# Attention scores computed head by head in row tiles and moved between partitions, in place of logits from mixed queries

## What is computed

```python
q, k = conv1x1_bn(xn, ...)            # 8 heads of 32 channels
v4 = conv1x1_bn(xn, ...)              # 8 heads of 128 channels
vl = depthwise_conv3x3(v4) * lv_s + lv_t
attn = einsum('bhid,bhjd->bhij', q, k) * 32 ** -0.5
attn = attn + ab[:, BIAS_IDXS]
attn = einsum('bhij,gh->bgij', attn, th1w) + th1b   # mixes the 8 heads
attn = softmax(attn)
attn = einsum('bhij,gh->bgij', attn, th2w) + th2b   # mixes them again
o = relu(einsum('bhij,bhjd->bhid', attn, v) + vl)
out = x + conv1x1_bn(o, pw, ...)
```

## Time and profile before

| | us |
|---|---|
| median of 3 runs (4534.37 to 4536.29) | 4536.19 |
| the profiled execution | 4534.58 |
| its span | 4532.8 |
| TensorE busy | 4505.5 (99%) |
| VectorE busy | 4197.4 (93%) |
| ScalarE busy | 3570.3 (79%) |
| GpSimd busy | 1360.9 (30%) |

### The profile page before, as it was taken

One profiled execution on the slowest core, in us unless ns is written; L12 is line 12 of the kernel. 1 busy time (PEld: TensorE's weight loads), 2 busy tenths in 40 slices (PEclk: granted clock), 3 DMA queues, 4 the chain that ended last, 5 costly groups with the idle time before them and its releaser, 6 DMA issues.

```text
span 4532.8 us, 108461 instructions
## 1 busy us (share of the span) xinstructions
PE 4505.5 (99%) x33666; PEld 4502.5 (99%) x33666; DVE 4197.4 (93%) x10015; ACT 3570.3 (79%) x8508; POOL 1360.9 (30%) x1288
## 2 busy tenths in 40 slices
PE   7999999999999999999999999999999999999999
PEld 7999999999999999999999999999999999999999
DVE  8999999999999999999999999999999999999998
ACT  7787877878778787787787877878778778787786
POOL 2323323323233232332322323323233232332322
PEclk9999999999999999999999999999999999999999
DMA  3322222223222232222322322223222232232222
GB/s 94 97 65 81 86 69 87 65 81 92 70 81 74 72 97 65 81 82 68 93 65 81 88 72 82 68 78 97 65 81 79 67 97 65 81 86 68 88 65 76
DMA packets 211502, 356.05 MB, mean 79 GB/s; under 512 B 15843, under 2 KB 132691, under 8 KB 211413
## 3 DMA queue, kind: packets, MB, share of 16 engines
q1 hardware_dynamic: 211478, 355.75, 27.3%
HBM read 199.71 MB, written 155.98 MB: 78 GB/s over the span
## 4 chain that ended last, share of the span: by engine, by line
PE 99%; DMA 0%; POOL 0%; DVE 0%; SPq 0%; ACT 0%; issue 0%; POOLq 0%; DVEq 0%
PE psA L293 45%; PE psA L426 15%; PE psL L293 13%; PE psM L293 10%; PE psM L404 9%; PE psL L404 7%; PE psA L306 0%; DMA qa<-in_wqkv 0%; SPq L254 0%; POOL xs L822 0%; DVE probs L730 0%; DMA by_key<-probs 0%; POOL wp_lo L863 0%; DVE q_lo L722 0%; ACT w_hi L443 0%
## 5 line engine op out<-in xcount | busy, mean ns | idle before, releaser
L700 DVE SCALAR_TENSOR_TENSOR psC<-vpad,par,psC 128x406 f32<-128x406 f32 x3072 | 1807.2, 635 | 0.0
L584 ACT ACTIVATE probs<-probs,nmax 112x196 f32<-112x196 f32 x1792 | 803.2, 451 | 128.8 <-DVE nmax L759 112.9
L293 PE MATMUL psA<-x_hi,w_lo 128*128 128x392 f32 x2304 | 794.9, 345 | 6.0 <-DVE x_lo L679 6.0
L293 PE MATMUL psA<-x_hi,w_hi 128*128 128x392 f32 x2304 | 785.7, 341 | 0.0
L293 PE MATMUL psA<-x_lo,w_hi 128*128 128x392 f32 x2304 | 785.1, 341 | 0.0
L426 PE MATMUL psA<-qa,shared 105*128 105x196 f32 x4096 | 690.9, 329 | 0.0
L426 PEld LDWEIGHTS psA<-qa,shared 105*128 105x128 f32 x4096 | 677.2, 190 | 0.4 <-DVE shared L794 0.3
L857 POOL TENSOR_TENSOR k_lo<-qk,k_hi 128x392 fp32r<-128x392 f32 x128 | 159.9, 1249 | 1636.4 <-ACT k_hi L490 1636.4
L722 DVE SCALAR_TENSOR_TENSOR q_lo<-qk,th,q_hi 128x392 fp32r<-128x392 f32 x1024 | 618.3, 632 | 2.0 <-ACT q_hi L486 1.9
L486 ACT ACTIVATE q_hi<-qk,th 128x392 fp32r<-128x392 f32 x1024 | 594.5, 618 | 2.1
L461 ACT ACTIVATE o_hi<-shared 128x392 fp32r<-128x392 f32 x512 | 271.6, 530 | 391.3 <-DVE shared L794 391.3
(11 more groups left out here) (85 smaller groups left out, 10723.1 us busy)
## 6 DMA issues: line engine op xcount, KB each, us to landing
by_key<-probs SPq DMA_DIRECT2D x512, 224.0 KB, 3.6
qa<-by_key SPq DMA_DIRECT2D x128, 448.0 KB, 4.3
qk<-by_key SPq DMA_DIRECT2D x128, 448.0 KB, 6.9
xs<-in_x SPq DMA_DIRECT2D x64, 588.0 KB, 3.8
shared<-in_x SPq DMA_DIRECT2D x64, 588.0 KB, 3.8
out<-shared SPq DMA_DIRECT2D x63, 588.0 KB, 3.0
qa<-in_wqkv SPq DMA_DIRECT2D x3, 768.0 KB, 7.1
stage_wp<-in_wp SPq DMA_DIRECT2D x1, 1536.0 KB, 9.6
```

Source lines behind the costliest of these rows:

```text
L293: last = nc.tensor.matmul(dst, w, r, start=(begin and n == 0), stop=(end and n == 2))
L584: nc.scalar.activation(row, row, ACT.Exp, bias=nmax[:, img, b:b + 1], scale=-1.0, accum_out=rowsum[:, img, b:b + 1]).then_inc(s_exp, 1)
L700: nc.vector.scalar_tensor_tensor(a if tap == 7 else sums, src, taps[:, c, TAPS[tap]:TAPS[tap] + 1], a if tap == 0 else sums, MUL, ADD).the ...
```

## The change

The first head mixing is no longer folded into the query. The query is scaled and written with its columns outermost. For each image and each group of 8 or 6 query columns (a unit; four per round) TensorE computes plain scores head by head: eight fp32 matmuls, each on 32 partitions (one head's channels), neighbouring ones on different quarters of the partitions and into different banks. The units stand between the V tiles 2 to 5. ScalarE and VectorE copy two banks of each unit to `scores`, whose partitions are (query column, query row) and whose free dimension holds head and key. SP then moves them within SBUF, eight DMAs per unit, to `by_head`, whose partitions are (head, query column). There one fp32 matmul of 392 columns with `kron1` mixes the heads for two query rows: 14 matmuls per round, the three projection tiles standing after the fourth, eighth and twelfth. `q_hi`, `q_lo`, `k_hi`, `k_lo` are gone.

The transposed V now goes to the buffer `qa` and is stored channel tile innermost; it comes back from DRAM straight into `vt`, whose weights attention times V reads with a stride of eight elements. The copies `head_major` and the reload of the row of ones are gone. The units of attention times V alternate the images, and all of them wait for the last copy of the mixed probabilities. The statistics for the next images, the centres and the convolution steps have new places; 22 convolution steps stand after the second reciprocal and up to eight between the additions.

```diff
-        q, k = qk[:, 0, :, :], qk[:, 2, :, :]
+        by_head = shared[0:HP, heads_at:heads_at + 2 * RES * PIX].rearrange("p (i n) -> p i n", i=2)
+        q, k = qk[:, 0, :, :], qk[:, 1, :, :]
+        scores = qa[0:WIDE, :].rearrange("p (i c h n) -> p i c h n", i=2, c=2, h=NH)
+        turned = qa[:, 0:TURNED].rearrange("p (i b n c) -> p i b n c", i=2, b=BLOCKS, c=VT)
...
+            def moves(t, u):
+
+                img, c = UNITS[u]
+                sp.wait_ge(s_score_a, 8 * t + 2 * u + 2)
+                sp.wait_ge(s_score_v, 8 * t + 2 * u + 2)
+                first_col = c * WIDE // RES
+                for h in range(NH):
+                    lo = h * RES + first_col
+                    sp.dma_start(by_head[lo:lo + score_rows(c) // RES, img, :].rearrange("w (b j) -> w b j", b=RES),
+                                 scores[0:score_rows(c), img, c, h, :]).then_inc(s_moved[u], 16)
+
+            def keys_in(t, img):
+
+                wait_alone(sp, s_vt_out[img], OUTS * (t + 1))
+                sp.wait_ge(s_logit_mm, 14 * t + (14 if img else 11))
+                for jc in range(2):
+                    sp.dma_start(vt[0:ROWS, img, jc, :],
+                                 by_key[img, jc * HALF:jc * HALF + ROWS, :]).then_inc(s_vt_in, 16)
...
-                turned_out(t)
-                ones_in(t)
-                keys_in(t)
+                if first:
+                    sp.wait_ge(s_bias, 1)
+                else:
+                    sp.wait_ge(s_olo, 8 * t)
+                    wait_alone(sp, s_av_mm, 8 * t)
+                for u in range(4):
+                    moves(t, u)
+                turned_out(t, 0)
+                turned_out(t, 1)
+                keys_in(t, 0)
+                keys_in(t, 1)
...
+            def head_scores(t, first, u):
+
+                img, c = UNITS[u]
+                if u:
+                    pe.wait_ge(s_score_a, 8 * t + 2 * u)
+                    pe.wait_ge(s_score_v, 8 * t + 2 * u)
...
+                at_ = img * PIX + c * WIDE
+                for kt in range(QT):
+                    for r in range(QUADS):
+                        part_ = slice(r * KD, (r + 1) * KD)
+                        mm = nc.tensor.matmul(score_bank(r)[0:score_rows(c), kt * PIX:(kt + 1) * PIX],
+                                              q[part_, kt, at_:at_ + score_rows(c)],
+                                              k[part_, kt, img * PIX:(img + 1) * PIX], start=True, stop=True)
+                mm.then_inc(s_score_mm, 1)
...
                     qkv_tile(m, 4 + m).then_inc(s_v_mm, 1)
+                    if m < 6:
+                        head_scores(t, first, m - 2)
...
-                else:
-                    project(t, 0, True)
-                    project(t, 1, True)
...
+                    if n % 7 == 0:
+                        pe.wait_ge(s_moved[2 * img], MOVES * (t + 1))
+                        pe.wait_ge(s_moved[2 * img + 1], MOVES * (t + 1))
                     if n >= 4:
                         pe.wait_ge(s_score, 28 * t + 2 * n - 6)
...
-                    for b in (b0, b0 + 1):
-                        for kt in range(QT):
...
+                    nc.tensor.matmul(logit_bank(n)[:, 0:2 * PIX], kron1[:, :, :].rearrange("p g i -> p (g i)"),
+                                     by_head[:, img, b0 * PIX:(b0 + 2) * PIX], start=True, stop=True
+                                     ).then_inc(s_logit_mm, 1)
...
+                    if n in (3, 7, 11) and not first:
...
+                        project(t, n // 4, True)
...
+                pe.wait_ge(s_vt_in, 64 * (t + 1))
+                pe.wait_ge(s_mix_sb, 14 * t + 14)
+                for u in range(8):
+                    n, img = divmod(u, 2)
...
+                            weights = vt[0:HALF, img, jc, :].rearrange("p (m c) -> p c m", c=VT)
...
+                for u in range(4):
+                    values(2 + u)
+                    score_copy(t, u, 0)
+                    score_copy(t, u, 1)
...
-                CENTRES = {1: 4, 3: 5, 9: 6, 11: 7}
+                CENTRES = {8: 4, 11: 5, 23: 6, 25: 7}
...
+                    if n in (7, 15) and not first:
+                        projected(t, n // 8)
...
+                    if use == 0:
+                        act.wait_ge(s_vt_out[0], OUTS * (t + 1))
+                        act.wait_ge(s_vt_out[1], OUTS * (t + 1))
+                        act.wait_ge(s_moved[2], MOVES * (t + 1))
...
+                convs(13)
...
+                for u in range(4):
+                    score_copies(u)
+                    convs(2 if u < 3 else 3)
...
+                    if n in (3, 7):
+                        turn(n // 4)
+                        convs(2)
+                    if n == 11:
+                        convs(5)
...
-                    convs(1)
                 convs(3)
                 dve.wait_ge(s_exp, 28 * t + 28)
                 nc.vector.reciprocal(rinv[:, 1, :], rowsum[:, 1, :]).then_inc(s_rinv, 1)
-                convs(3)
-                convs(64)
+                convs(22)
...
+                    if u == 6:
+                        convs(64)
...
                     if u:
                         low(u - 1)
+                    convs(1)
```

More of the change, by code:

```diff
@@ L87, in build @@
         proj = sb("proj", [P, CT, COLS])
[L89 to L92, removed]
+        qk = sb("qk", [P, 2, QT, COLS])
+        unused = sb("unused", [P, 2, RUN])
         qa = sb("qa", [P, 4 * RES * HP])
@@ L103, in build @@
         stage_wp = sb("stage_wp", [P, VT * COLS])
-        q_lo = over("q_lo", [P, 2 * RES, QT, HP], VT // 2 * ACC)
-        shared = sb("shared", [P, VT * ACC + 4 * DH + GAP + CT * COLS])
+        shared = sb("shared", [P, VT * ACC + 4 * DH + CT * COLS])
         psA = ctx.enter_context(nc.psum_tensor("psA", [P, 2, BANK], f32))
@@ L387, in step @@
                         pe.wait_ge(s_stat, 4 * (t + 1))
                         group_sums(t + 1)
-                if not first:
-                    project(t, 2, True)
-                pe.wait_ge(s_ones_in, 16 * (t + 2))
+                    if n in (3, 7, 11) and not first:
+                        if n == 7 and not last:
+                            pe.wait_ge(s_gs, t + 2)
+                        project(t, n // 4, True)
+                if first:
+                    pe.wait_ge(s_ones_in, 16)
@@ L448, in _, with conv_centre @@
             weights_high(2)
-            def conv_centre(t, c):
+            def conv_centre(t, first, c):
                 act.wait_ge(s_v_sb, VT * t + c + 1)
+                if not first and c % 2 == 0:
+                    act.wait_ge(s_olo, 8 * (t - 1) + c + 2)
                 if c >= VT // 2:
-                    act.wait_ge(s_logit_mm, 14 * t + c - 3)
+                    act.wait_ge(s_logit_mm, 14 * t + c - 2)
                 src = vpad[:, c, PITCH + 1:PITCH + 1 + ACC_ROWS * PITCH].rearrange("p (r w) -> p r w", w=PITCH)
@@ L527, in step @@
                 values(0)
-                if not first:
-                    act.wait_ge(s_olo, 8 * t)
-                conv_centre(t, 0)
+                conv_centre(t, first, 0)
                 values(1)
-                conv_centre(t, 1)
+                conv_centre(t, first, 1)
+                query_or_key(0)
+                query_or_key(1)
+                query_or_key(2)
+                query_or_key(3)
                 if first:
@@ L854, in step @@
             def step(t, first, last):
-                for kt in range(QT):
-                    wait_alone(pool, s_khi, 2 * t + kt + 1)
-                    nc.gpsimd.tensor_tensor(k_lo[:, kt, :], k[:, kt, :], k_hi[:, kt, :].bitcast(f32),
-                                            SUB).then_inc(s_klo, 1)
                 if first:
```

290 lines of the change are left out of this document (106 added, 184 removed).

## The result

The changed kernel takes 5390.12 us (median; 5385.06 to 5392.25) against 4535.78 of the kernel before in the same runs: 1.188 times as long, 95% interval 1.186 to 1.190, or 854 us, 13.6 us for each of 63 rounds. Forecast were 5090 us and a range of 4620 to 6400. The sign, the wait for the moves as the main loss, and the range came out. Of the two waits that were forecast there is one, and 300 us more were lost than the sum had.

The account below looks back on a forecast made before the run. TensorE, busy 99%, was taken to bound the kernel at 70.2 us per round. The new round, 73.4 us plus 5.6 of waits, makes 79.0, 8.8 more; 63 such add 554 us, giving 5090, range 4620 to 6400.

Parts of the forecast that it names:

- TensorE's list was the bound before, and the change takes little from it: TensorE's work per round: 70.2 us before, 69.2 after, a saving of one microsecond.
- only neighbouring matmuls overlap: Head scores: a second fp32 pass waits for its first, so the scores take 6.4 us per round.
- Two waits for the moves: TensorE waits at the first and eighth mixing, 2.4 and 3.2 us, with moves at 100 GB/s.
- the rival by partitions: Move rate proportional to destination partitions: 50 GB/s gives 103.6 us rounds, 60 to 65 gives 97, 6200 us; chance 0.26.
- the rival with a long pause: Moves at 50 GB/s, late by 14.7 and 15.5 us; clock at 0.50 adds 3 us: rounds of 107, 6850 us.
- From the first mixing to the next round's first tile 47.8 us: Stretch from first mixing until VectorE's add 6 releases the next tile: 47.8 us, against 43.7 for TensorE alone.
- The forecast sign, a TensorE wait of 3 to 4 us at the turn of the round: Before the next round's first tile, TensorE waits 3 to 4 us, released by VectorE's add.
- VectorE covers it: Strided V weight load, between nothing and 2.8 us per round, taken as nothing because VectorE's wait hides it.
- the walk: Step-by-step timing of TensorE, VectorE and ScalarE from the first mixing on; each V unit costs VectorE 1.51 us.
- moves hidden: Moves faster than 130 GB/s cause no wait: rounds of 73.4 us, 4736 us in all; chance 0.24.
- Serial tiles: Score tiles one after another, 10.6 us, leave only a 2.5 us wait: rounds of 80.2, 5160 us; within the forecast's 0.36.
- Faster: Score row tiles fully concurrent, 2.7 us, and moves hidden: rounds of 69.7 us, 4500 us; chance 0.11.

Follow-up runs that it names:

- run 7: Changed kernel with projections 0 and 1 ahead of the first mixing, projection 2 behind mixing 6, ten more convolution steps before the first score row: 5110.85 us, 1.127.
- run 4: Changed kernel whose 32 transfers, from the second round on, keep their packet count but carry a quarter of the bytes: 5190.89 us, 1.145.
- Run 10: Changed kernel with 36 more matmuls a round, whose results nobody reads, ahead of the first mixing: 5318.78 us, 1.173.
- run 1: Changed kernel with the weights of attention times V read packed, from neighbouring elements, instead of with a stride: 5371.6 us, 1.185.
- run 3: Changed kernel moving only head 0 of eight from the second round on, 4 transfers per round in place of 32: 4744.72 us, 1.046.
- run 5: Changed kernel with all head-score matmuls reading partitions 0 to 31, so that they share a row group and run serially: 5587.33 us, 1.233.
- run 11: Changed kernel with the last score unit's eight moves issued by ScalarE's queue, the other 24 by the sync queue: 5495.91 us, 1.212.
- 2: Changed kernel with the earlier kernel's V path: packed transposes, raw buffers, four ScalarE copies, packed weights: 5355.15 us, 1.181.
- 8: Changed kernel with projections 0 and 1 ahead of the first mixing and the earlier kernel's V path together: 5188.79 us, 1.145.

## Why the prediction was right, and where its sum was off

*TensorE's list was the bound before, and the change takes little from it.* Right. 12 tiles and scores take 23.7 us, predicted 25.6; the four units take 3.5 us (0.86 each), not 6.4, but each tile behind one takes 1.81 us in place of 1.61 (2037.16 to 2038.97), 0.8 in all, which the sum didn't have. What failed is that because of the two passes "only neighbouring matmuls overlap": in the timeline all four tiles are at work in either pass. The Trainium skill (TensorE: Matmul & The Clock Gate, Part 3) has 3.07 for 512 columns, by which the prediction estimated 3.5 us; the trace agrees.

*Two waits for the moves, 2.4 and 3.2 us.* The sum, 5.6, against 7.2 to 7.7 and no second one. TensorE is at the first mixing 1.9 us earlier than reckoned (the scores), and units 0 and 1 land 30.7 us after the first tile, not 28.0, though the rate over all four units was close: 2.46 MB in 24.3 us of issue, 101 GB/s, against 100 taken, and units 2 and 3 land after 41.4 us (run 7), not 40.3. That the rate came out was luck, as its reason was another. I took it from the number of partitions; run 4 shows the issue of 32 transfers as the cap and the bytes as a tail of 6 us behind it, which I had at 0.7. From 27.6 GB/s for four partitions in the Trainium skill (SBUF — State Buffer, Door 1) the prediction estimated 55 for eight; the windows between 2050.4 and 2062.4 show 101 to 133, with several transfers to different partitions under way, so the rival by partitions falls.

*The half clock.* Missing in the sum: 2.2 us a round. I had it for the rival with a long pause, from the earlier trace rows, and not for my own pauses of 2 to 3 us; the pause became one of 7. Run 10 shows the mechanism.

*From the first mixing to the next round's first tile 47.8 us.* Measured 52.1 (2056.00 to 2108.06). 2.2 of the 4.3 are the clock. The other 2.0 are in the tail: by TensorE's count the strided weights make 15.6 us of attention times V, where the sum had 13.4; by VectorE's, as run 1 shows, the low half beside GpSimd's `x_lo` makes 15.3. Each alone brings the 2 us, and each hides the other. The forecast sign, a TensorE wait of 3 to 4 us at the turn of the round for VectorE's add, isn't there: TensorE is busy for all 15.62 us, so it is the load that VectorE's tail hides behind, and "VectorE covers it" failed for a load that costs 5.0 us a round, above my bound of 2.8. Taking it away gains 18 us in all, but only because of the second failed term, VectorE's tail: the changed order brings `x_lo` for the next images (2.7 us on GpSimd) beside the low halves, and the walk had only waits for semaphores. In run 1 VectorE needs 12.6 us from its first add to the end of the one that the next tile waits for, against 10.8 by the walk. The transposes' 3.4 us were not priced at all and cost nothing that shows.

The ledger for one round: 79.0 predicted, +1.6 wait, -1.9 scores, +2.2 clock, +2.0 tail makes 82.9, and the round above has 82.94; of the 0.7 by which the mean round is longer, 0.5 are the wait (7.7 on the mean). The rival *moves hidden*, 4736, was met by run 3 within 9 us, by luck: a round of run 3 takes 73.40 us against 73.4, but from 23.5 up to the first mixing in place of 25.6, and 49.9 behind it in place of 47.8, so that the scores' error and the tail's cancel. *Serial tiles* would have been 5587, not 5160 (run 5): 2.8 us a unit as priced, but the granted clock falls in the last ones, so that TensorE is at the first mixing after 36.2 us and not 29.8; the second wait of 2.5 isn't there, and the tail is 49.9 again. *Faster* was never near: even with moves hidden the kernel is at 4745.

What stays open: what besides the issue holds the moves back (run 11); whether the same bytes in fewer transfers would land earlier, which no run tried; and why the granted clock falls under serial matmuls on 32 rows.

## What to carry to other kernels

A transfer between partitions in many small DMAs had two prices here, one for each issue, which a quarter of the payload didn't lower, and a landing time behind the last, which it did; work out both against the first instruction that needs the data, and keep independent work to stand in that gap. A pause on TensorE can also cost what comes after it, at half clock: 2.2 us behind 7.2 here. Undoing one part of a change can gain next to nothing (1, 2: 18 and 35 us) because another engine's work has the same length, and undoing two can be worse than one (8): a part is worth what the next wait leaves.

## What the hardware showed that I had not expected

- Four row tiles of fp32 matmuls overlap in both passes: 16 passes of 196 columns in 0.86 us, against 2.8 on one row group at full clock.
- A low half on VectorE (two inputs in SBUF) that met a 2.68 us GpSimd operation took 2.57 us instead of 0.56 (run 1). It shows as a longer instruction, not as a wait; in the changed kernel one took 1.61 us beside the same operation.
- The granted clock fell to 0.50 with TensorE busy all the time, under serial matmuls on 32 rows (run 5, busy for 5.40 of 5.40 us).
- A weight load with a stride of eight fp32 elements took 336 ns against 190 to 200 packed, and the pass 0.244 us against 0.166; a transpose that writes with that stride 3.75 us against 2.04.
- An SBUF to SBUF transfer of 8 or 6 partitions took 0.76 us to issue on the sync or ScalarE's queue at 64 to 86 KB and at a quarter of that, and about 1.8 us on GpSimd's, gaps between groups of four included.
